# Scores of 16-column heads as products of 64 rows, with half as many masked copies of the keys and one set of three score banks

## The chip, the cores and the metric

The kernel runs on one core of one Trainium2 chip. The metric is the device time of one execution in microseconds (us), from the runs of this case. The engines are TensorE (PE in the profile, its weight loads PEld), VectorE (DVE), ScalarE (ACT), GpSimd (POOL) and SyncE (SP), which here only issues transfers.

## The reference, cut to what matters

64 images of 96x96 are cut into 36 patches each, so the tower works on 2304 tokens of D = 192 columns. It has an embedding, a first attention with 12 heads of 64 columns, an attention and MLP pair (`attn2`, `mlp`), a third attention (`attn3`) and a mixture of experts. The change touches `attn2` and `attn3` alone. Both have 12 heads of 16 columns over the 36 tokens of one image:

```
def _attn_branch(xp, w_qkv, w_proj, b_proj, ...):       # attn2, once per half of the images
    qkv = (xp @ w_qkv).reshape(B2, N, 3, H, hd).transpose(2, 0, 3, 1, 4)     # H = 12, hd = 16, N = 36
    a = softmax(einsum('bhnd,bhmd->bhnm', q, k) * hd ** -0.5)
    o = einsum('bhnm,bhmd->bhnd', a, v).transpose(0, 2, 1, 3).reshape(B2, N, C)
    o = o @ w_proj + b_proj
def _L1_attn_ref(x, w_qkv, b_qkv, w_proj, b_proj):      # attn3
    ...
    scores = einsum('bhnd,bhmd->bhnm', q, k) * scale + bias[None]            # bias: distance times slope
    attn = softmax(scores)
    out = einsum('bhnm,bhmd->bhnd', attn, v)
    ...
    return out @ w_proj.T + b_proj
```

## The kernel before

`narrow_stage` writes both stages, from one text; `attn2` has a normalisation in front (`prenorm`) and no bias on the scores, `attn3` has the bias and a normalisation behind (`postnorm`). Each engine runs its own program in order, and semaphores join them.

**Tiling.** A unit is two images (72 tokens), a group is four units (WIDE = 288 tokens). There are 32 units and 8 groups in a stage. The queries and keys of a group are projected into tiles with the columns of a head on 16 rows: `q_a` and `keys_a` hold heads 0 to 7 (128 rows), `q_b` and `keys_b` heads 8 to 11 (the rows 0 to 63 of a tile of 128, the rest zero).

**Scores of a unit.** A head uses 16 of the 128 rows of the array, so the keys stand in masked copies: copy h of `keys_a` is the keys with all rows but those of head h made zero. One product of the query (stationary, 64 columns of tokens, 36 of them of the image) with all copies (moving, 8 x 36 = 288 columns) then gives the scores of eight heads. `scores(k)` (L1020 on) does this for both images, a = 0 and 1, into the rows 0 to 63 and 64 to 127 of one bank of PSUM, then the same for `keys_b` with 4 x 36 = 144 columns. All matmuls here are f32 and appear in the trace as two records each. The masked copies are made by `mask_keys_a` on ScalarE (L1155 in `attn2`, L1157 in `attn3`), one instruction per copy, four in the step after the projection of the keys and four in the next; for the first group by one instruction of VectorE (`mask_keys_a0`, L1266 or L1267), and those of `keys_b` always by VectorE (`mask_keys_b`, the same lines).

**The order of a step.** The stage has 35 steps. In step k TensorE does `scores(k)`, `mix(k - 3)` (probabilities by values, L1060), a part of the next group's projections (j = k mod 4: transposes of the tokens L983 and L984; projections L994 to L998 of q_a and keys a; then q_b and keys b; then the values L1013 to L1017 in three parts), `turn(k - 2)` (four transposes of the probabilities, L1043) and `project_out` of the tiles that are ready (L1069, L1070). VectorE does `take_scores(k)` first: in `attn2` the row maximum (L1296) and its subtraction (L1298), both from PSUM; in `attn3` it adds the bias (L1290), takes the maximum (L1294), and GpSimd subtracts (L938). ScalarE takes the exponential (L1172), VectorE the row sums (L1305) and their reciprocals (L1310), GpSimd multiplies (L931), TensorE turns, ScalarE copies the turned probabilities out (`copy_turned`, L1179) and, after mix, z (L1189). In ScalarE's queue of a step stand: exponential of k - 1, copy of z, the work for the projections, copy of the turned, and last the mask copies.

**Buffers.** Scores have two banks (2 and 3), turned probabilities two (4 and 5), by the parity of k; so `scores(k)` waits until unit k - 2 is taken, and `turn(k)` until unit k - 2 is copied out. The first part of a group's values waits for all mask copies, since they read the bank that it writes.

## Time and profile before

| what | us |
|---|---|
| median of 3 timed runs | 906.39 (905.71 to 907.11) |
| the profiled execution, its own time | 909.75 |
| its span from first to last instruction | 908.0 |
| mean granted clock of TensorE | 0.965 |
| TensorE busy | 831.0 (92%) |
| VectorE busy | 543.1 (60%) |
| ScalarE busy | 461.0 (51%) |
| GpSimd busy | 410.3 (45%) |

The span is that of one execution under the profiler; what lies between it and the execution's time (1.75 us) is start and end. Busy times are unions of durations. The ends of matmuls are modelled, so the time that a matmul really holds TensorE is read from the start of one to the start of the next.

### The profile page before, as it was taken

What the parts mean: (1) busy time and instruction counts of PE and PEld (TensorE: products, weight loads), DVE (VectorE), ACT (ScalarE), POOL (GpSimd) and SP (SyncE); (2) the same over time, 40 slices, a digit from 0 to 9 for tenths busy, and PEclk for the clock granted to TensorE, in tenths of its full rate; (3) what the DMA queues carried; (4) which work ended last, traced back from release to release, by engine and by line L of the source; (5) the groups of instructions that cost most, each with busy time, mean ns of one, the idle gap of its engine ahead of it and who ended that gap; (6) DMA issues with size and microseconds to landing.
All of it is one profiled execution on the core that took longest, in us unless ns stands there. A gap on an engine that the chain in (4) does not pass through costs nothing. (4 is left out here: it accounts for less than half of the span.)

```text
span 908.0 us, 20892 instructions
## 1 busy us (share of the span) xinstructions
PE 831.0 (92%) x7511; PEld 748.5 (82%) x7511; DVE 543.1 (60%) x1466; ACT 461.0 (51%) x1150; POOL 410.3 (45%) x489
## 2 busy tenths in 40 slices
PE   9899999999998798998999988988979999999982
PEld 8889998899997577776999986776757899899972
DVE  2236555556665788884773326888875622466645
ACT  0346565555644587874345526877735221255533
POOL 1535444344444444432441225777851355244445
PEclk9989999999999999996999998999969999999997
DMA  9810111111110131214400002633200011233243
GB/s 315 255 50 21 22 35 37 31 31 30 38 36 2 33 67 25 37 19 123 74 1 1 1 26 42 138 68 68 42 7 2 29 62 63 76 103 100 83 149 116
DMA packets 103940, 55.75 MB, mean 61 GB/s; under 512 B 67264, under 2 KB 94512, under 8 KB 103840
## 3 DMA queue, kind: packets, MB, share of 16 engines
q1 hardware_dynamic: 98032, 43.04, 19.9%
q0 software_dynamic: 3792, 7.84, 2.5%
q10 hardware_dynamic: 2016, 3.54, 1.3%
q8 instruction: 62, 1.02, 0.5%
q14 instruction: 38, 0.31, 0.1%
HBM read 29.81 MB, written 13.97 MB: 48 GB/s over the span
## 5 line engine op out<-in xcount | busy, mean ns | idle before, releaser
L931 POOL TENSOR_TENSOR attn_prob<-attn_prob,attn_recip 100x432 f32<-100x432 f32 x64 | 58.6, 915 | 75.5 <-DVE attn_recip L1310 75.2
L450 POOL TENSOR_TENSOR attn_prob_x<-attn_prob,attn_recip 100x864 f32<-100x864 f32 x32 | 52.7, 1646 | 52.7 <-DVE attn_recip L759 52.7
L1886 POOL DMA_INDIRECT results<-moe_hid_shared x43 | 41.3, 960 | 58.4 <-ACT moe_hid_shared L2101 58.4
L1596 ACT ACTIVATE mlp_hid<-psum,columns 128x384 f32<-128x384 f32 x72 | 38.1, 579 | 41.4 <-PE psum L96 41.4
L1060 PEld LDWEIGHTS psum<-attn_prob_t,attn_values 108*64 108x64 f32 x1024 | 39.3, 142 | 13.6 <-ACT attn_prob_t L1179 7.8
L1060 PE MATMUL psum<-attn_prob_t,attn_values 108*64 108x36 f32 x1024 | 41.6, 228 | 6.1 <-ACT attn_prob_t L1179 4.1
L2076 ACT ACTIVATE moe_silu<-psum 128x384 f32<-128x384 f32 x36 | 17.7, 491 | 56.6 <-PE psum L107 56.6
L1033 PE MATMUL psum<-attn_keys_a,attn_q_a 128*64 128x288 f32 x256 | 45.8, 437 | 0.0
L1043 PE MATMUL psum<-ident,attn_prob 100*108 100x100 f32 x256 | 35.8, 265 | 9.5 <-POOL attn_prob L931 9.5
L1172 ACT ACTIVATE attn_prob<-attn_prob 100x432 f32<-100x432 f32 x64 | 36.5, 571 | 15.5 <-POOL attn_prob L938 14.7
L1305 DVE TENSOR_REDUCE attn_row_sum<-attn_prob 100x12 f32<-100x432 f32 x64 | 38.0, 594 | 8.1 <-ACT attn_prob L1172 7.9
L1549 PE MATMUL psum<-mlp_w_dn_s,mlp_hid 128*128 128x192 f32 (+2 forms) x306 | 42.6, 290 | 0.0
L436 POOL TENSOR_TENSOR attn_rstd<-attn_var_eps,neg_half 128x1 f32<-128x1 f32 x18 | 10.3, 570 | 71.3 <-DVE attn_var_eps L771 71.3
L686 ACT ACTIVATE attn_z_t<-psum 128x432 f32<-128x432 f32 (+2 forms) x32 | 16.2, 507 | 50.8 <-PE psum L566 50.7
L1549 PEld LDWEIGHTS psum<-mlp_w_dn_s,mlp_hid 128*128 128x128 f32 x306 | 42.0, 191 | 0.0
L938 POOL TENSOR_TENSOR attn_prob<-attn_prob,attn_row_max 100x432 f32<-100x432 f32 x32 | 29.2, 912 | 25.6 <-DVE attn_row_max L1294 25.6
L1964 PE MATMUL psum<-w_dn_shared,moe_hid_shared 128*128 128x192 f32 x216 | 36.3, 327 | 4.7 <-DVE moe_hid_shared L2251 3.3
L1964 PEld LDWEIGHTS psum<-w_dn_shared,moe_hid_shared 128*128 128x128 f32 x216 | 35.2, 190 | 5.4 <-DVE moe_hid_shared L2251 3.6
L576 PE MATMUL psum<-w_o,attn_z_t 128*128 128x192 f32 x216 | 38.7, 329 | 0.9 <-ACT attn_z_t L686 0.6
L1449 POOL TENSOR_TENSOR mlp_rstd<-mlp_var_eps,neg_half 128x1 f32<-128x1 f32 x18 | 10.6, 590 | 63.3 <-DVE mlp_var_eps L1665 63.3
L734 DVE TENSOR_SCALAR attn_k_diag<-psum,columns 64x288 f32<-64x288 f32 x48 | 25.0, 524 | 22.8 <-PE psum L508 15.4
L2251 DVE TENSOR_TENSOR moe_hid_shared<-psum,moe_silu 128x384 f32<-128x384 f32 x36 | 20.0, 555 | 30.8 <-PE psum L107 30.7
(473 smaller groups left out, 2853.5 us busy)
## 6 DMA issues: line engine op xcount, KB each, us to landing
embed_patches<-in_x SPq DMA_DIRECT2D x8, 768.0 KB, 17.2
sorted_rows<-mlp_pad_zeros SPq DMA_DIRECT2D x1, 4214.0 KB, 15.7
moe_hid_shared<-sorted_rows SPq DMA_DIRECT2D x43, 98.0 KB, 2.0
attn_v<-attn_v_tok SPq DMA_DIRECT2D x16, 216.0 KB
attn_values<-attn_v_tok SPq DMA_DIRECT2D x96, 27.0 KB
side_raw_a<-in_w_gu_dram SPq DMA_DIRECT2D x8, 288.0 KB, 3.3
side_raw_b<-in_w_gu_dram SPq DMA_DIRECT2D x16, 144.0 KB, 3.4
h_rows<-results SPq DMA_DIRECT2D x6, 288.0 KB, 5.3
```

The source lines that it names most:

```text
L450: nc.gpsimd.tensor_tensor(prob_x[k % 2][:, :, :, :], prob[k % 3][:, :, :].rearrange("p h (a n) -> p h a n", a=1) .to_broadcast([QP, HEADS, ...
L576: last = nc.tensor.matmul(out_ps, z_t[:, c, at:at + P], w_o[:, c, :], start=(c == 0), stop=(c == chunks - 1))
L931: nc.gpsimd.tensor_tensor(pr, pr, recip[k % 2][:, :].rearrange("p (h a) -> p h a", a=1) .to_broadcast([QP, HEADS, SEQ]), ALU.mult).then_in ...
L1033: last = nc.tensor.matmul(ps[64 * a:64 * a + 64, h0:h1, :], q[g % 2][:, at:at + 64], keys[g % 2][:, :, at:at + SEQ], start=True, stop=True)
L1043: last = nc.tensor.transpose(bank(4 + k % 2)[0:3 * SEQ, n * P:n * P + QP], flat[:, n * 3 * SEQ:(n + 1) * 3 * SEQ], ident[0:QP, 0:QP])
L1060: last = nc.tensor.matmul(ps[r:r + 64, n // 2, a * SEQ:(a + 1) * SEQ], v[:, n, :], prob_t[k % 2][:, n, a, :], start=True, stop=True)
L1172: nc.scalar.activation(prob[k % 3][:, :, :], prob[k % 3][:, :, :], ACT.Exp).then_inc(S["exp_done"], 1)
L1305: nc.vector.tensor_reduce(row_sum[:, :], prob[k % 3][:, :, :], axis=AX.X, op=ALU.add).then_inc(S["sum_ready"], 1)
L1549: last = nc.tensor.matmul(bank(3 + t)[:, 0:w.shape[1]], hid_step(n)[:, t * MT:(t + 1) * MT], w, start=(n == 0), stop=(n == 17), skip_group ...
L1596: nc.scalar.activation(hid_step(n), bank(n % 3)[:, 0:MW], ACT.Gelu, bias=b_up[:, c:c + 1]).then_inc(S["gelu_done"], 1)
L1886: nc.gpsimd.indirect_dma_start(out=results, out_offset=bass.IndirectOffsetOnAxis(ap=x_in[j % x_ring][:, D:D + 1].bitcast(U32), axis=0), in ...
L1964: last = nc.tensor.matmul(bank(4 + n % 2)[:, 0:D], hid_of(i)[:, c, t * P:(t + 1) * P], w_dn_shared[:, c, :], start=(c == 0), stop=(c == sh ...
```

## The change

The copies of `keys_a` are masked with period 64: copy h (0 to 3) keeps the rows of head h and of head h + 4, so there are four copies of 288 tokens and not eight. The rows 0 to 63 and 64 to 127 are then products of their own, of 64 rows by 64 columns of the array and 144 moving columns, for each of the two images: four products, of which each uses one quarter of the array. Heads 0 to 3 (rows 0 to 63), 4 to 7 (rows 64 to 127) and 8 to 11 (`keys_b`, products of 128 rows as before) go to three banks of their own, 2, 3 and 4. There is one such set, so `scores(k)` waits until unit k - 1 is taken. The turned probabilities keep bank 5 alone, so `turn(k)` waits until unit k - 1 is copied out. The reads of VectorE go over three banks with 144 columns each. A mask of four columns is made from that of eight at the start, by one more instruction of VectorE.

```diff
@@ -837,7 +837,7 @@
...
-    keys_a = [sb(f"keys_a{p}", [P, 8, WIDE]) for p in range(2)]
+    keys_a = [sb(f"keys_a{p}", [P, 4, WIDE]) for p in range(2)]
...
@@ -857,11 +857,10 @@
     def bank(b):
...
-    def scores_ps(k):
-        return bank(2 + k % 2)[:, 0:HEADS * SEQ].rearrange("p (h n) -> p h n", h=HEADS)
-
-    def turned_ps(k):
-        return bank(4 + k % 2).rearrange("p (g a n) -> p g a n", g=4, a=2)
+    scores_ps = psum[:, 2 * BANK:5 * BANK].rearrange("p (s n) -> p s n", s=3)[:, :, 0:4 * SEQ].rearrange(
+        "p s (h n) -> p s h n", h=4)
+
+    turned_ps = bank(5).rearrange("p (g a n) -> p g a n", g=4, a=2)
...
@@ -1000,7 +999,7 @@
...
         def values(g, n):
...
-                pe.wait_ge(S["keys_a_made"], 8 * g + 8)
+                pe.wait_ge(S["keys_a_made"], 4 * g + 4)
...
@@ -1021,26 +1020,28 @@
...
-                pe.wait_ge(S["keys_a_made"], 8 * g + 8)
+                pe.wait_ge(S["keys_a_made"], 4 * g + 4)
...
-            if k >= 2:
-                pe.wait_ge(S["scores_taken" if bias_hk is not None else "shifted"], k - 1)
-            ps = scores_ps(k)
-            for q, keys, h0, h1 in ((q_a, keys_a, 0, 8), (q_b, keys_b, 8, HEADS)):
-                for a in range(2):
-                    at = u * UNIT + a * SEQ
-                    last = nc.tensor.matmul(ps[64 * a:64 * a + 64, h0:h1, :], q[g % 2][:, at:at + 64],
-                                            keys[g % 2][:, :, at:at + SEQ], start=True, stop=True)
+            if k >= 1:
+                pe.wait_ge(S["scores_taken" if bias_hk is not None else "shifted"], k)
+            for r, a in ((0, 0), (64, 1), (0, 1), (64, 0)):
+                at = u * UNIT + a * SEQ
+                nc.tensor.matmul(scores_ps[64 * a:64 * a + 64, r // 64], q_a[g % 2][r:r + 64, at:at + 64],
+                                 keys_a[g % 2][r:r + 64, :, at:at + SEQ], start=True, stop=True)
+            for a in range(2):
+                at = u * UNIT + a * SEQ
+                last = nc.tensor.matmul(scores_ps[64 * a:64 * a + 64, 2], q_b[g % 2][:, at:at + 64],
+                                        keys_b[g % 2][:, :, at:at + SEQ], start=True, stop=True)
...
         def turn(k):
...
-            if k >= 2:
-                pe.wait_ge(S["turned_copied"], k - 1)
+            if k >= 1:
+                pe.wait_ge(S["turned_copied"], k)
...
-                last = nc.tensor.transpose(bank(4 + k % 2)[0:3 * SEQ, n * P:n * P + QP],
+                last = nc.tensor.transpose(bank(5)[0:3 * SEQ, n * P:n * P + QP],
...
@@ -1088,7 +1089,7 @@
...
-                keep_going(nc, bank(4), ident, out_ws[0][:, 0:2, :], 2)
+                keep_going(nc, bank(5), ident, out_ws[0][:, 0:2, :], 2)
...
@@ -1176,7 +1177,7 @@
...
-            nc.scalar.activation(prob_t[k % 2][:, :, :, :], turned_ps(k)[0:3 * SEQ, :, :, 0:SEQ], ACT.Copy
+            nc.scalar.activation(prob_t[k % 2][:, :, :, :], turned_ps[0:3 * SEQ, :, :, 0:SEQ], ACT.Copy
...
         def copy_z(k):
@@ -1218,9 +1219,9 @@
...
-                mask_keys_a(g, range(4))
+                mask_keys_a(g, range(2))
...
-                mask_keys_a(g, range(4, 8))
+                mask_keys_a(g, range(2, 4))
...
@@ -1270,7 +1271,7 @@
         def mask_keys_a0():
...
-                          None if qk_bias is None else qk_bias[:, 1:2]).then_inc(S["keys_a_made"], 8)
+                          None if qk_bias is None else qk_bias[:, 1:2]).then_inc(S["keys_a_made"], 4)
...
         def mask_keys_b(g):
...
@@ -1278,25 +1279,27 @@
...
             else:
...
-            spread_masked(keys_b[g % 2][0:DB, :, :], bank(0)[DB:P, 0:WIDE], head_mask[DB:P, 4:8],
+            spread_masked(keys_b[g % 2][0:DB, :, :], bank(0)[DB:P, 0:WIDE], head_mask[DB:P, :],
...
         def take_scores(k):
...
-            ps, pr, mx = scores_ps(k)[0:QP], prob[k % 3][:, :, :], row_max[k % 2][:, :]
+            ps, pr, mx = scores_ps[0:QP], prob[k % 3][:, :, :], row_max[k % 2][:, :]
+            pr_sets = pr.rearrange("p (s h) n -> p s h n", s=3)
             if bias_hk is not None:
-                nc.vector.tensor_tensor(pr, ps, bias_hk[:, :, :], ALU.add).then_inc(S["scores_taken"], 1)
+                nc.vector.tensor_tensor(pr_sets, ps, bias_hk[:, :, :].rearrange("p (s h) n -> p s h n", s=3), ALU.add
+                                        ).then_inc(S["scores_taken"], 1)
...
             else:
-                nc.vector.tensor_reduce(mx, ps, axis=AX.X, op=ALU.max).then_inc(S["max_done"], 1)
+                nc.vector.tensor_reduce(mx.rearrange("p (s h) -> p s h", s=3), ps, axis=AX.X, op=ALU.max).then_inc(S["max_done"], 1)
...
-                ins = nc.vector.tensor_tensor(pr, ps, mx.rearrange("p (h a) -> p h a", a=1)
-                                              .to_broadcast([QP, HEADS, SEQ]), ALU.subtract)
+                ins = nc.vector.tensor_tensor(pr_sets, ps, mx.rearrange("p (s h a) -> p s h a", s=3, a=1)
+                                              .to_broadcast([QP, 3, 4, SEQ]), ALU.subtract)
...
         def sum_up(k):
@@ -2647,7 +2650,7 @@
...
-        head_mask, k_bias_by_head3 = sb("head_mask", [P, 8]), sb("k_bias_by_head3", [P, 8])
+        head_mask, k_bias_by_head3 = sb("head_mask", [P, 4]), sb("k_bias_by_head3", [P, 4])
...
@@ -2682,6 +2685,7 @@
             def prepare(S, ssb):
...
+                head_mask8 = ssb("head_mask8", [P, 8])
...
@@ -2720,8 +2724,11 @@
...
                 def vector_start(dve):
...
-                    nc.vector.tensor_reduce(head_mask[:, :], ident[:, :].rearrange("p (h n) -> p h n", h=8),
+                    nc.vector.tensor_reduce(head_mask8[:, :], ident[:, :].rearrange("p (h n) -> p h n", h=8),
...
+                    dve.wait_ge(S["head_mask_ready"], 1)
+                    nc.vector.tensor_tensor(head_mask[:, :], head_mask8[:, 0:4], head_mask8[:, 4:8], ALU.add
+                                            ).then_inc(S["head_mask_ready"], 1)
...
@@ -2739,7 +2746,7 @@
                 def scale_columns(dve):
...
-                    dve.wait_ge(S["head_mask_ready"], 1)
+                    dve.wait_ge(S["head_mask_ready"], 2)
...
```

## Rows read from the trace of the kernel before

**Rows 1.** The page, busy time of the engines over the span.
```profile
PE 831.0 (92%) x7511; PEld 748.5 (82%) x7511; DVE 543.1 (60%) x1466; ACT 461.0 (51%) x1150; POOL 410.3 (45%) x489
```
**Rows 2.** Windows, one in `attn2` and one in `attn3`.
```profile
core 0: us, PE busy (x) PEld busy (x) DVE busy (x) ACT busy (x) POOL busy (x), PEclk, DMA share, GB/s
331.00:345.00 14.00, 13.71 (x160) 11.19 (x156) 12.63 (x32) 11.68 (x35) 6.35 (x9) 1.00 0.24 36
611.00:626.00 15.00, 13.63 (x158) 11.16 (x156) 14.12 (x30) 11.03 (x28) 10.83 (x13) 1.00 0.30 56
```
**Rows 3.** Timeline of TensorE in `attn2`: start, union of durations, instructions merged.
```profile
336.79 0.51 PE L1043 MATMUL psum<-ident,attn_prob 100*108 100x100 f32 x4
...
337.23 0.71 PE L1033 MATMUL psum<-attn_keys_a,attn_q_a 128*64 128x288 f32 x4
...
337.76 0.41 PE L1033 MATMUL psum<-attn_keys_b,attn_q_b 128*64 128x144 f32 x4
...
338.01 0.61 PE L1060 MATMUL psum<-attn_prob_t,attn_values 108*64 108x36 f32 x16
...
338.55 0.40 PE L994 MATMUL psum<-ring_a_hi,w_qkv_a_hi 128*128 128x288 f32 x1
...
343.84 0.51 PE L1043 MATMUL psum<-ident,attn_prob 100*108 100x100 f32 x4
...
344.19 0.51 PE L1069 MATMUL psum<-w_o,attn_z_t 128*128 128x192 f32 x2
...
344.95 0.71 PE L1033 MATMUL psum<-attn_keys_a,attn_q_a 128*64 128x288 f32 x4
```
**Rows 4.** Timeline around a mask batch: ScalarE, TensorE; last line `attn3`.
```profile
337.39 0.39 ACT L1179 ACTIVATE attn_prob_t<-psum 108x288 f32<-108x288 f32 x1
...
337.68 1.65 ACT L1155 ACTIVATE attn_keys_a<-psum,head_mask 128x288 f32<-128x288 f32 x4
...
339.22 0.57 ACT L1172 ACTIVATE attn_prob<-attn_prob 100x432 f32<-100x432 f32 x1
...
339.32 0.51 PE L1043 MATMUL psum<-ident,attn_prob 100*108 100x100 f32 x4
...
340.02 0.30 PEld L1069 LDWEIGHTS psum<-w_o,attn_z_t 128*128 128x128 f32 x2 [0.39 <-ACT attn_z_t L1189]
...
585.62 2.04 ACT L1157 ACTIVATE attn_keys_a<-psum,k_bias_by_head,head_mask 128x288 f32<-128x288 f32 x4
```
**Rows 5.** Waits of the weight loads, 303-415 and 551-671 us: total, times, longest.
```profile
PEld psum L1013 <- ACT attn_keys_a L1155: 1.9, 3, 0.9
...
PEld psum L1069 <- ACT attn_z_t L1189: 1.5, 4, 0.4
...
PEld psum L1043 <- POOL attn_prob L931: 4.4, 3, 1.7
PEld psum L1013 <- ACT attn_keys_a L1157: 4.4, 6, 1.3
...
PEld psum L1069 <- ACT attn_z_t L1189: 4.2, 5, 0.9
```
**Rows 6.** Instructions that write the key copies, VectorE: min/median/max ns, first and last start.
```profile
L1266 DVE TENSOR_TENSOR attn_keys_a<-psum,head_mask x1: 2558/2558/2558, 295.9 to 295.9; 128x2304 f32<-128x2304 f32 x1
...
L1266 DVE TENSOR_TENSOR attn_keys_b<-psum,head_mask x8: 1359/1359/1361, 298.5 to 398.5; 64x1152 f32<-64x1152 f32 x8
```
**Rows 7.** Timeline of TensorE at the two stages' starts: second part of the values.
```profile
300.02 0.31 PE L1013 MATMUL psum<-w_qkv_a_hi,ring_a_hi 128*108 128x192 f32 x1 [0.76 <-DVE attn_keys_b L1266]
...
548.25 0.32 PE L1013 MATMUL psum<-w_qkv_a_hi,ring_a_hi 128*108 128x192 f32 x1 [0.21 <-DVE attn_keys_b L1267]
```
**Rows 8.** Timeline: unit 7 taken, scores of unit 8; a wait in `attn3`.
```profile
330.08 0.61 DVE L1298 TENSOR_TENSOR attn_prob<-psum,attn_row_max 100x432 f32<-100x432 f32 x1
...
330.58 0.71 PE L1033 MATMUL psum<-attn_keys_a,attn_q_a 128*64 128x288 f32 x4
...
627.23 0.55 PE L1043 MATMUL psum<-ident,attn_prob 100*108 100x100 f32 x4 [1.39 <-POOL attn_prob L931]
```

## Prediction

> **What bounds the kernel now.** First the page's busy shares [rows 1]: TensorE works 92% of the span, VectorE 60%. That average hides the two stages that the change touches, `attn2` (about 294 to 430 us) and `attn3` (about 541 to 684 us), so the windows come next [rows 2]. There TensorE is busy 13.7 of 14 and 13.6 of 15 us, VectorE 12.6 of 14 and 14.1 of 15, ScalarE 11.7 and 11.0. A group of four units takes 14.4 us in `attn2` (scores of unit 8 at 330.58, of unit 12 at 344.95 [rows 8, 3]), and the three engines hand work to each other inside it. So the reader must look for who ends TensorE's waits, in the waits of its weight loads [rows 5], and for what lies on the way to them, in the timeline of one step [rows 3, 4]. Those waits, and the matmul time between them, are what the change can win.
>
> **Scores.** Today a unit's scores are two f32 products of 288 columns and two of 144, each recorded twice. Their pairs (a = 0, 1: two halves of the columns of the array) run abreast: the 288-column ones hold 0.53 us (337.23 to 337.76), the others 0.25 (337.76 to 338.01) [rows 3], 0.78 in all, 0.05 of it the uncovered first weight load (0.53 against twice 0.24). The change makes the first part four products of 64 rows and 144 columns. If all four run abreast they take what the 144-column pair takes, 0.24. The trace has no product of 64 rows, so this is bounded by the nearest rows: 0.24 four abreast, 0.48 two abreast, 0.96 one at a time. I take 0.24, since two products abreast with different moving data cost nothing today, and four half-height ones read no more rows and columns per moment. What is added is a change of shape between the quarters and the last two products. Its price, from the nearest rows: four transposes followed by a full product hold 0.35 us (343.84 to 344.19), followed by scores 0.44 (336.79 to 337.23) [rows 3], so 0.09, and 0.05 for the uncovered load: 0.14. Bounds 0 (if 64 and 128 rows don't count as different shapes) and 0.28 (a change among half-width shapes twice as dear); I take 0.15. New scores: 0.05 + 0.24 + 0.15 + 0.24 = 0.68, so 0.10 less a unit. For 64 units that is 6.4 us; TensorE sets the pace in some six of ten of them (elsewhere a wait behind takes the time back): **-3.8 us**, with bounds -9.6 (0.25 a unit in six of ten, no price for the switch) and +7.7 (two abreast, +0.15 a unit, on the path in eight of ten because TensorE is then later than the rest).
> That a change of shape costs 0.09 here agrees with the Trainium skill (TensorEngine Tiling, Key Properties), by which a change of tiling mode drains the array and a change of tile does not; this rule speaks against the change, and it has no figure. The Trainium skill (TensorE: Matmul & The Clock Gate, Part 3) gives a speedup of 3.07 for four row tiles, which no row here shows; an estimate from that page would make the quarters 0.31, the scores 0.75 and the whole term -1.2 (0.03 x 64 x 0.6) instead of -3.8.
>
> **Masks on ScalarE.** L1155 and L1157 write eight masked copies of the keys in each of seven groups, in two batches of four; the change makes them two batches of two. A batch of four holds 1.65 us in `attn2` (337.68 on), so two copies fewer take some 0.8 off. In `attn3` the batch is 2.04 [rows 4]; it loses some 1.0. In sum 14 x 0.8 + 14 x 1.0 = 25 us of ScalarE. Little of it is TensorE's: rows 4 show the way, mask batch, exponential 339.22, a copy of z, out projection 340.02, and TensorE's weight load had been waiting only 0.39 us. So the gain is capped by the waits that end on masks or on what is queued behind them [rows 5]: 1.9 + 1.5 us in `attn2`, 4.4 + 4.2 in `attn3`, 12.0 together. The wait for the normalised probabilities (4.4 in `attn3`) also hangs in part on an exponential behind a mask batch. VectorE, busy 0.90 and 0.94 of the windows, takes some back. I take six tenths of 12.0: **-7.2 us**, bounds -12 and -3.
>
> **Start of a stage.** The first group's masks are one VectorE instruction of 2304 columns, 2.56 us in `attn2`; of 1152 columns it is 1.36 [rows 6], 1.20 less. In `attn2` the second part of the values waits 0.76 for the key masks behind it (300.02), and the statistics that x_hat needs come after those on VectorE, so all 1.2 counts; in `attn3` TensorE came only 0.21 before them (548.25) [rows 7], so 0.2. **-1.4 us**; bounds -2.4 and -0.5.
>
> **One set of score banks.** scores(k) now waits for unit k-1 to be taken (L1298 in `attn2`, L1290 in `attn3`), before for k-2. Behind it in TensorE's queue stand mix, the projections and the transposes of k-2, for which ScalarE's and GpSimd's queues wait. I compared the end of each taking with the start of the next scores: of 62 pairs, 21 have less than 0.4 us between, twelve of them under 0.1. A usual one: taking ends 330.69, scores start 330.58 [rows 8]: 0.2 us of stall with the signal. The deep ones (scores up to 1.1 us ahead) come right before a wait for GpSimd, as the one at 627.23 of 1.39 us [rows 8], which absorbs them. Some seven stalls of 0.2: **+1.5 us**, bounds 0 and +10.5 (below).
>
> **At nothing.** One bank for turned probabilities: the copy out ends 337.78, the next transposes start 339.32 [rows 4]; the smallest such distance is 1.3 us; if ScalarE were that much later the transposes would wait by the rest. VectorE's score reads keep 432 columns, split over three banks; I take no change: L1298 takes 0.61 us for 432 columns [rows 8], 1.4 ns each, and L1266, which reads with one dimension more, 1.2 ns each [rows 6]. The extra mask addition at the very start lies beside the embedding loads. More instructions on TensorE (six products a unit for four) issue inside the stream: mix sends 16 in 0.54 us [rows 3].
>
> **Sum.** -3.8 - 7.2 - 1.4 + 1.5 = -10.9. The profiled execution took 909.75 us (span 908.0, 1.75 around it), so it would take 898.9; it stands 3.4 above the median of the timed runs, 906.39, and the same difference from that gives 895.5.
>
> **Rivals.** (1) The quarters do not run four abreast: slower. Two abreast: +7.7; masks only -5, as TensorE comes later to the waits; start -1.4, banks +1: +2.3, 908.7. One at a time: +0.62 a unit, about 935. It decides from 0.14 us more per unit than today ((1.4 + 7.2 - 1.5) over 64 x 0.8). For: no 64-row product in the trace. Against: today's pairs, with two streams of keys, overlap fully. (2) TensorE and VectorE in lockstep: the single set of banks eats what the masks give, since TensorE now arrives earlier at scores that VectorE has not taken. The 21 near pairs at 0.5 each: +10.5 for +1.5, 904.5. For: VectorE 0.94 busy in `attn3`. Against: VectorE's own start in those steps (row sum after exponential) lay behind the same mask batches. (3) The better case: no price for the switch (-9.6), masks -9, start -1.4, banks +1: -19, 887.4.
>
> **Numbers.** Forecast 0.55 (its own range 892 to 900); (1) 0.15; (2) 0.17; (3) 0.13. A measurement of this kernel can't tell 0.2% (1.8 us) from no change. Faster: 0.55 + 0.13 + 0.10 of (2) = 0.78; within 0.2%: 0.06 of (2) and 0.01 of (1) = 0.07; slower 0.15. The range goes from (3) to two abreast: 887 to 909.
>
> **What would show it.** The scores of a unit from first product to mix: 0.68 us right; 0.9 or more is (1). The start of the products after the quarters tells the switch. Mask batches of 0.9 and 1.1 us, and TensorE's waits for L1155 or L1157 nearly gone; if a group's pace in `attn2` stays 14.4 and TensorE waits for L1298 or L1290 in front of scores, it is (2). Transposes must not wait for L1179. Outside the two stages nothing may change. Wrong I would be by the quarters, or by a pace that VectorE alone sets.

## The result, and the profile after

| | before | changed |
|---|---|---|
| median of the session in which it was first timed, us | 907.22 | 902.24 |
| the profiled execution, us | 909.75 | 900.14 |
| its span, us; granted clock | 908.0; 0.965 | 898.4; 0.964 |

The changed kernel's median is that of 11 executions: a twelfth took 1054.58 us at a clock of 0.722 and is left out here and below. The ratio of the changed kernel to the one before is 0.9946 (95% interval 0.9926 to 0.9966), so 4.9 us less (3.1 to 6.7). Two later sessions gave 0.9949 (0.9928 to 0.9969) and 0.9964 (0.9947 to 0.9981). It is faster, and inside the range, but by 4.9 us and not by the forecast 10.9. The two profiled executions differ by more, 9.6 us. Two things have to be explained: what took the other 6 us, and why these two numbers disagree. In the rows below numbers of lines are those of the changed kernel: quarters L1030, the last two score products L1034, `turn` L1044, `mix` L1061.

The page's busy shares, and the two windows of [rows 2]:
```profile
PE 824.2 (92%) x7767; PEld 744.7 (83%) x7767; DVE 540.4 (60%) x1467; ACT 440.0 (49%) x1094; POOL 409.6 (46%) x489
```
```profile
core 0: us, PE busy (x) PEld busy (x) DVE busy (x) ACT busy (x) POOL busy (x), PEclk, DMA share, GB/s
331.00:345.00 14.00, 13.40 (x174) 11.00 (x172) 12.67 (x33) 10.14 (x29) 6.10 (x10) 1.00 0.24 36
611.00:626.00 15.00, 13.04 (x150) 10.94 (x150) 13.90 (x31) 8.32 (x22) 11.17 (x14) 0.89 0.27 46
```
ScalarE lost 21 us of work. TensorE's busy time fell in both windows, but in the second its clock is 0.89, where it was 1.00 in [rows 2].

One unit's scores in TensorE's timeline, to be held against [rows 3]:
```profile
335.68 0.51 PE L1044 MATMUL psum<-ident,attn_prob 100*108 100x100 f32 x4
336.12 0.48 PE L1030 MATMUL psum<-attn_keys_a,attn_q_a 64*64 64x144 f32 x8
336.53 0.47 PE L1034 MATMUL psum<-attn_keys_b,attn_q_b 128*64 128x144 f32 x4
336.82 0.61 PE L1061 MATMUL psum<-attn_prob_t,attn_values 108*64 108x36 f32 x16
```
The four quarters and the change of shape behind them hold 0.41 us (336.12 to 336.53), the other two products with the uncovered load 0.29: 0.70, against 0.78 before. Eight quarter records of about 0.3 us each lie within 0.48 us, so they run abreast (in the raw records their starts are 6 to 7 ns apart).

The writers of the key copies, by tile, and a batch on ScalarE in either stage (timeline):
```profile
L1156 ACT ACTIVATE attn_keys_a<-psum,head_mask x28: 482/494/504, 309.8 to 397.6; 128x288 f32<-128x288 f32 x28
...
L1267 DVE TENSOR_TENSOR attn_keys_a<-psum,head_mask x1: 1358/1358/1358, 295.9 to 295.9; 128x1152 f32<-128x1152 f32 x1
```
```profile
381.02 0.89 ACT L1156 ACTIVATE attn_keys_a<-psum,head_mask 128x288 f32<-128x288 f32 x2
```
```profile
577.99 1.07 ACT L1158 ACTIVATE attn_keys_a<-psum,k_bias_by_head,head_mask 128x288 f32<-128x288 f32 x2
```
These are the forecast 0.9, 1.1 and 1.36 us, for 1.65, 2.04 and 2.56 in [rows 4, 6].

Now who is waited for. The waits of the weight loads in `attn3` (541 to 661 us, which is the stretch of [rows 5] moved with the kernel), then those of the matmuls in `attn2` (303 to 415 us): total, times, longest.
```profile
PEld psum L1044 <- POOL attn_prob L930: 5.6, 7, 1.5
PEld psum L1061 <- DMA attn_values<-attn_v_tok: 3.5, 2, 2.0
...
PEld psum L1030 <- DVE attn_prob L1292: 1.3, 4, 0.5
```
```profile
PE psum L1030 <- DVE attn_prob L1301: 4.2, 8, 1.2
PE psum L1061 <- ACT attn_prob_t L1180: 3.7, 6, 1.4
```
No wait for L1158 over 0.4 us is left. New are the waits of the quarters for VectorE (L1301, L1292), which come from the single set of score banks. Those for the values' transfers are longer than before (here the row of the stretch of [rows 5]):
```profile
PEld psum L1060 <- DMA attn_values<-attn_v_tok: 2.6, 2, 1.5
```
For GpSimd the stretches don't compare well, since one wait of 3.3 us at the stage's end lies outside both. Over the whole stage (541 to 675 us) that wait holds 7.7 us before and 8.9 after.

**Where the 9.6 us lie.** Read from the starts of scores in the two traces, seven groups of `attn2` (units 0 to 28) take 101.60 us before and 101.67 after: no gain. Ahead of them 1.2 us are won (the start of the stage) and behind them 1.2 (units 28 to 31, where a stretch of half clock at 407 us stands before and not after). Seven groups of `attn3` take 105.77 and 101.09, and units 28 to 31 there 10.0 and 8.9. One more us lies between the two stages, where the change does nothing: the half-clock stretches that begin at 417 us last 17.1 us before and 13.7 after.

### The profile page after: what moved, and what is told of

Its sections match the earlier page's. It is cut to its first block and busy times, and to the rows that moved or that the text cites. A ratio compares the mean times of both kernels' runs of the same rounds, so it can differ in the third digit from the quotient of the medians.

```text
span 898.4 us, 21351 instructions
## 1 busy us (share of the span) xinstructions
PE 824.2 (92%) x7767; PEld 744.7 (83%) x7767; DVE 540.4 (60%) x1467; ACT 440.0 (49%) x1094; POOL 409.6 (46%) x489
## 5 line engine op out<-in xcount | busy, mean ns | idle before, releaser
L1061 PEld LDWEIGHTS psum<-attn_prob_t,attn_values 108*64 108x64 f32 x1024 | 39.5, 142 | 14.3 <-ACT attn_prob_t L1180 8.9
L1061 PE MATMUL psum<-attn_prob_t,attn_values 108*64 108x36 f32 x1024 | 41.6, 228 | 7.6 <-ACT attn_prob_t L1180 4.6
L1044 PE MATMUL psum<-ident,attn_prob 100*108 100x100 f32 x256 | 35.8, 265 | 8.4 <-POOL attn_prob L930 8.4
L436 POOL TENSOR_TENSOR attn_rstd<-attn_var_eps,neg_half 128x1 f32<-128x1 f32 x18 | 10.2, 568 | 71.3 <-DVE attn_var_eps L771 71.3
L553 PE MATMUL psum<-ident,attn_prob_x 100*72 100x100 f32 x384 | 38.4, 249 | 0.0
```

Source lines behind the costliest of these rows:

```text
L553: last = nc.tensor.transpose(bank(3 + p)[0:UNIT, n * P:n * P + QP], prob_x[k % 2][:, 4 * p + n, :, :].rearrange("p a n -> p (a n)"), ident ...
L1044: last = nc.tensor.transpose(bank(5)[0:3 * SEQ, n * P:n * P + QP], flat[:, n * 3 * SEQ:(n + 1) * 3 * SEQ], ident[0:QP, 0:QP])
L1061: last = nc.tensor.matmul(ps[r:r + 64, n // 2, a * SEQ:(a + 1) * SEQ], v[:, n, :], prob_t[k % 2][:, n, a, :], start=True, stop=True)
```

## The experiments

Ratios are to the kernel before, run on the same chip in the same session; 0.001 is 0.9 us. "Clock" is the median over a kernel's executions of the mean granted TensorE clock.

| kernel | ratio (95% interval) | median us | clock |
|---|---|---|---|
| changed, first session | 0.9946 (0.9926 to 0.9966) | 902.24 | 0.964 |
| e5, e14: changed again | 0.9949, 0.9964 | 903.20, 902.62 | 0.962 |
| e1 masks halved | 0.9968 (0.9950 to 0.9987) | 902.32 | 0.9665 |
| e2 wait for k-1 | 1.0033 (1.0010 to 1.0056) | 909.77 | 0.967 |
| e3 changed, masks doubled | 1.0040 (1.0020 to 1.0059) | 911.59 | 0.961 |
| e4 filler, 16 places | 0.9965 (0.9948 to 0.9982) | 902.70 | 0.970 |
| e6 masks halved and wait | 1.0000 (0.9981 to 1.0018) | 907.00 | 0.964 |
| e7 take earlier | 0.9974 (0.9951 to 0.9997) | 904.51 | 0.960 |
| e8 filler, 4 places | 0.9937 (0.9918 to 0.9957) | 900.41 | 0.9645 |
| e9 quarters last | 0.9964 (0.9937 to 0.9991) | 903.22 | 0.9675 |
| e10 before, filler, 4 places | 1.0012 (0.9994 to 1.0031) | 906.89 | 0.972 |
| e11 filler, 9 places | 0.9968 (0.9944 to 0.9993) | 903.19 | 0.9725 |
| e12 filler, 6 places | 0.9938 (0.9918 to 0.9958) | 899.04 | 0.9685 |
| e13 filler, 1 place | 0.9961 (0.9945 to 0.9977) | 901.70 | 0.967 |

### e1, e2 and e6: the masks alone, the wait alone, both, without quarters

e1 is the kernel before with four of ScalarE's eight copies from the third group on, which is six of the seven groups that ScalarE masks; the other four heads then use keys of an earlier group, so the output is another. e2 is the kernel before with the wait of the changed one. e6 has both edits.
```diff
-                mask_keys_a(g, range(4))
+                mask_keys_a(g, range(4 if g < 2 else 2))
...
-                mask_keys_a(g, range(4, 8))
+                mask_keys_a(g, range(4, 8 if g < 2 else 6))
...
-            if k >= 2:
-                pe.wait_ge(S["scores_taken" if bias_hk is not None else "shifted"], k - 1)
+            if k >= 1:
+                pe.wait_ge(S["scores_taken" if bias_hk is not None else "shifted"], k)
```


> The kernel before, with ScalarE writing only four of the eight copies of keys_a from the third group on (the other four stay as the group two before left them, so those heads' scores are of old keys). The scores keep their shape and their two banks. By the sum of the prediction the masks are worth -7.2 of the -10.9 us; six of seven groups have them here, so -6. The clock theory (what TensorE wins in these stages turns into idle stretches, in which its clock falls to half, and half of the win goes back) expects -3 to -4 on the median and a wide spread of the executions, as that of the changed kernel (895.6 to 907.4). The theory that the single set of banks takes the win expects the full -6, since both sets are here.

> The kernel before, with scores(k) waiting for unit k-1 to be taken instead of k-2: the wait of a single set of banks, without the quarters and with all eight mask copies. The prediction's term was +1.5 us (bounds 0 and +10.5). The bank theory expects +4 to +6, which would explain the gap between -10.9 forecast and some -5 measured; the clock theory expects +0 to +2.

> The kernel before with half of ScalarE's masked copies left out from the third group on (four heads' keys are those of an earlier group) and with scores(k) waiting until unit k-1 is taken; products of 128 rows as before. Theory lockstep: the one set of score banks gives back in attn2 what the masks won, so a clean group there (units 20 to 24) takes 13.8 us against 13.26 with the masks alone, TensorE idle ahead of the scores of its first unit, and the whole is 1 to 3 us under the kernel before. Theory clock: the wait alone is worth little, and the loss comes with the quarters; a clean group takes 13.3 and the whole is 5 to 6 us under before, as near as the mean clock lets it. The difference to the changed kernel is what the quarters do: forecast 3.8 us, under lockstep 1 to 2, since time saved ahead of a wait for VectorE lengthens the wait.

Measured: -2.9 us for the masks (-4.5 to -1.2), +3.0 for the wait (0.9 to 5.1), 0.0 for both (-1.7 to 1.6); the two add up. No theory has all three: e1 came out as the clock theory said, e2 between the two, and of e6 lockstep had the group (13.8 us) and its place for the wait, but not the whole. The masks are worth half of my -6 for six groups (-7.2 for seven), and the wait is twice my +1.5. A clean group of `attn2` at full clock (from the scores of unit 20 to those of unit 24) shows both. In order before, e1, e6, changed kernel, each as the window of the group and the row of the scores that end it:
```profile
374.65:388.33 13.68, 13.25 (x155) 10.88 (x154) 12.12 (x28) 11.18 (x32) 5.64 (x8) 1.00 0.23 32
...
388.33 0.71 PE L1033 MATMUL psum<-attn_keys_a,attn_q_a 128*64 128x288 f32 x4
```
```profile
371.13:384.39 13.26, 13.15 (x155) 10.83 (x154) 11.85 (x29) 9.95 (x28) 5.65 (x8) 1.00 0.24 33
...
384.39 0.71 PE L1033 MATMUL psum<-attn_keys_a,attn_q_a 128*64 128x288 f32 x4
```
```profile
371.55:385.36 13.81, 13.07 (x155) 10.99 (x155) 12.16 (x29) 10.28 (x29) 5.65 (x8) 1.00 0.23 32
...
385.36 0.71 PE L1033 MATMUL psum<-attn_keys_a,attn_q_a 128*64 128x288 f32 x4 [0.49 <-DVE attn_prob L1298]
```
```profile
374.05:387.79 13.74, 12.77 (x171) 10.57 (x171) 12.18 (x29) 10.24 (x29) 5.64 (x8) 1.00 0.23 33
...
387.79 0.48 PE L1030 MATMUL psum<-attn_keys_a,attn_q_a 64*64 64x144 f32 x8 [0.65 <-DVE attn_prob L1301]
```
The kernel before takes 13.68 for this group, TensorE idle 0.43 of it. The halved masks make it 13.26, with TensorE busy all but 0.11 of it. With the single set of banks it is 13.81: TensorE comes to a group's first scores before VectorE has taken the last unit of the group ahead, which stands in VectorE's queue behind a mask of 1.36 us and the normalisation of two token tiles. The quarters take 0.3 off TensorE's busy time, and the wait grows from 0.49 to 0.65; the group is 13.74. So in a clean group of `attn2` the whole change is worth nothing. Over seven groups the wait costs 1.7 us in `attn2` (98.20 in e1, 99.89 in e6) and 1.3 in `attn3` (103.86 and 105.20).

In `attn3` the masks' waits did go, and others grew. The waits of e1's weight loads, 546 to 666 us, against [rows 5]:
```profile
PEld psum L1043 <- POOL attn_prob L931: 11.1, 8, 3.3
...
PEld psum L1060 <- DMA attn_values<-attn_v_tok: 3.8, 2, 2.3
...
PEld psum L1013 <- ACT attn_keys_a L1157: 1.6, 2, 1.3
```
The wait for L1157 fell from 4.4 to 1.6 and that for the copy of z from 4.2 to nothing, 7.0 in all. The one for GpSimd rose from 4.4 to 11.1, but 3.3 of it is the wait at the stage's end that lay outside the stretch before: over the whole stage it is 7.7 before and 11.1 here, 3.4 more. The values' transfers took 1.2 more. So 4.6 of the 7.0 us came back as other waits.

### e3: the changed kernel with eight masked copies

ScalarE writes four further copies that nobody reads.
```diff
-                mask_keys_a(g, range(2))
+                mask_keys_a(g, (0, 1, 4, 5))
...
-                mask_keys_a(g, range(2, 4))
+                mask_keys_a(g, (2, 3, 6, 7))
```


> The changed kernel, with ScalarE writing eight copies in each group again (four of them are read by nobody). What is left is quarters, single set of banks and the shorter first mask. By the prediction's sum: -3.8 - 1.4 + 1.5 = -3.7 us against before. The bank theory expects no gain or a loss (-1.4 - 3.8 + 5 = 0); the clock theory -1 to -3.

Measured +3.6 us (1.8 to 5.3), outside what either theory expected: the quarters are worth nothing that can be measured when the masks are not halved. With e2 and e6 it makes a square, all with the wait for k-1, in us against before:

| | products of 128 rows | quarters and shorter start |
|---|---|---|
| eight copies | +3.0 (e2) | +3.6 (e3) |
| four copies | 0.0 (e6) | -4.3 (changed, mean of its three ratios) |

The quarters with the shorter start give 4.3 us where the masks are halved and -0.6 where they aren't; halving the masks gives 3.0 without quarters and 7.9 with them (without quarters in six of the seven groups alone). Each cell is uncertain by nearly 2 us, and e3's clock is the lower, 0.961 for e2's 0.967, so the size of this effect is rough and the clock's part in it is not separated. A reading that fits is that time saved on one engine of the three counts only when the next in line is out of the way as well.

### e9: what the change of shape costs

The two products of 128 rows go first, the quarters last.


> The changed kernel with the order of a unit's score products turned round: the two products of 128 rows first, then the four quarters, then mix. The number of changes between 64 and 128 rows ahead of a next product goes from one a unit (quarters to the other scores; the way in costs as before) to two. If a change costs the 0.11 to 0.16 us that was read between quarters and scores, a unit gets about 0.1 longer and the whole 2 to 6 us longer than the changed kernel, where TensorE sets the pace. If the gap after the quarters is not a price of the change of shape but of the order (a weight load that finds the array full), the unit takes 0.70 as before and the time stays.

Timeline of one unit (here L1030 is the pair of `keys_b`, L1034 the quarters):
```profile
384.62 0.47 PE L1030 MATMUL psum<-attn_keys_b,attn_q_b 128*64 128x144 f32 x4
385.02 0.47 PE L1034 MATMUL psum<-attn_keys_a,attn_q_a 64*64 64x144 f32 x8
385.43 0.66 PE L1061 MATMUL psum<-attn_prob_t,attn_values 108*64 108x36 f32 x16
```
The scores hold 0.81 us, 0.40 and 0.41, for 0.70: the pair that held 0.29 ahead of `mix` holds 0.40 ahead of the quarters. So one more change costs 0.11 us, whichever way it goes. Over 64 units that would be 7 us, yet the clean group takes only 13.84 instead of 13.74: TensorE waited 0.35 us for VectorE in front of the next group instead of 0.65. That is the same cushion seen from the other side. The whole is within its uncertainty of the changed kernel, of which no execution was timed beside it; the expected 2 to 6 us are neither shown nor excluded.

### e7: taking the scores earlier

```diff
-                if j == 2:
+                if j == 3:
                     pre_norm(g + 2)
```


> The changed kernel with one piece of VectorE's queue moved in attn2: the two normalising instructions L1250 go from a group's third step to its fourth, behind the taking of scores, so that the last unit of a group is taken 0.7 us earlier. Lockstep: TensorE's wait of 0.65 us ahead of the first scores of a group goes, a clean group takes 13.1 us instead of 13.74, and the whole is 3 to 5 us under the changed kernel. Clock: the idle is gone too, so the mean clock rises by 0.002 or more. If neither holds the pace stays 13.7 and the wait stands elsewhere (the transposes of x then wait for L1250).

The wait in front of the scores went, and the other one that I had named came:
```profile
389.76 0.30 PE L982 MATMUL psum<-ident,attn_x_hat 128*128 128x128 f32 x1 [0.54 <-DVE attn_x_hat L1250]
```
The clean group fell from 13.74 only to 13.31, and seven groups of the stage together took 101.8 us, as in the changed kernel (101.7); the whole did not gain (904.51 us, its clock 0.960). The expected 3 to 5 us and the higher clock did not come: moving one piece of VectorE's queue moved the wait to another place.

### The clock: e5, e14, e4, e8, e10, e11, e12, e13

The changed kernel's executions spread from 895.6 to 907.4 us (31 executions, three sessions) and follow their own mean clock: correlation -0.85, 0.69 us for each 0.001. For the kernel before (112 executions, four sessions) it is -0.87 and 0.52 us. The median clocks are 0.963 and 0.970. Read from the two fitted lines at a clock of 0.968, before takes 907.7 and the changed kernel 899.2: 8.5 us less, not 4.9.

The 8.5 us are less certain than they look: they compare kernels by straight lines through their executions, and 0.968 is above the clock of most executions of the changed kernel.

In the profile a lower mean is a few more stretches at half the clock (0.50, 1.2 GHz for 2.4). This is one of them, in the changed kernel, as windows and as the timeline ahead of it:
```profile
346.00:349.40 3.40, 1.77 (x32) 1.05 (x30) 1.88 (x5) 3.06 (x8) 1.40 (x2) 1.00 0.36 34
349.40:352.80 3.40, 3.40 (x15) 3.37 (x16) 2.84 (x9) 1.31 (x7) 1.27 (x2) 0.50 0.29 56
```
```profile
346.58 0.47 PE L1034 MATMUL psum<-attn_keys_b,attn_q_b 128*64 128x144 f32 x4
348.48 0.66 PE L1061 MATMUL psum<-attn_prob_t,attn_values 108*64 108x36 f32 x16 [1.43 <-ACT attn_prob_t L1180]
```
TensorE waits 1.43 us for the turned probabilities, is busy 1.77 of these 3.40 us, and then runs 3.4 us at 0.50. The kernel before has this wait too, of 1.35 us, and there the clock stays up:
```profile
346.40:349.80 3.40, 2.05 (x20) 1.45 (x22) 1.88 (x5) 2.86 (x7) 2.11 (x4) 1.00 0.36 37
349.80:353.20 3.40, 3.20 (x36) 2.86 (x38) 3.27 (x10) 2.33 (x9) 0.52 (x1) 1.00 0.29 29
```
At this place the clock fell in all six profiles of kernels with quarters and no filler (changed, e3, e5, e7, e9, e14) and in one of four without quarters (e2; not in before, e1, e6).

The test is work that takes the place of the idle time and computes nothing that is used, f32 products of 128 x 384 into a bank that is free. e8 has two of them at each of four waits, e13 at this one alone, e10 puts e8's into the kernel before, e4 has one in every group ahead of the mix of its third unit; e11 and e12 add further places.
```diff
+            if k >= 1:
+                pe.wait_ge(S["z_copied"], k)
+            if k in ((10, 14) if prenorm else (0, 8)):
+                keep_going(nc, bank(6), ident, out_ws[0][:, 0:2, :], 2)
             if u == 0:
                 pe.wait_ge(S[f"values_ready{g % 2}"], 16 * 9 * (g // 2 + 1))
             pe.wait_ge(S["turned_copied"], k + 1)
-            if k >= 1:
-                pe.wait_ge(S["z_copied"], k)
```
The filler writes the bank of z, so the wait for the copy of z moves ahead of it, in every step.


> The changed kernel once more, unaltered, on the chip of the three kernels beside it, so that they are compared with it in one session. Median 900 to 904 us, 4 to 6 us under the kernel before. In its profile each stretch of half clock inside the two stages should follow an idle time of TensorE, and executions with a lower mean granted clock should be longer by 1 to 2 us for each 0.002.

> The changed kernel, with one f32 product of 384 columns that nobody reads, in the bank of z, ahead of mix's wait for the turned probabilities in every fourth step (the one in which TensorE waits for ScalarE behind the rounding of the tokens). It takes 0.32 us twice of TensorE, in a place where it waits up to 1.4 us. If the clock takes the gain: fewer half-clock stretches inside the stages, mean granted clock above 0.966 in most executions, the spread narrower and the median 3 to 5 us below the changed kernel (897 to 899). If the clock has nothing to do with it: the same as the changed kernel or up to 3 us slower (16 fillers at 0.2).

> The changed kernel with two extra full products, 0.65 us together, at four places alone, each ahead of a wait in which TensorE stood idle for 0.96 to 1.73 us (the mixes of units 10 and 14 in attn2, 0 and 8 in attn3); no work of the kernel is changed. Clock: the stretches of half clock at 349 and 585 us go, the group that holds them gets 1.5 us shorter, the mean clock rises from 0.964 to 0.967 or more, and the whole is 2 to 4 us under the changed kernel with a smaller spread. Lockstep: no change, within 1 us of the changed kernel, since the waits stay as long.

> The changed kernel with two extra products at one place alone, ahead of the wait of 1.43 us in which TensorE stands idle in attn2 (the mix of unit 10). With the extra products at four places this group took 14.7 us instead of 16.25. If the half clock behind that wait is the price, this one place gives 1.0 to 1.8 us of the whole, 901 to 902, and the group of units 12 to 16 takes 14.7; if the gain of the four places came from elsewhere, the group stays at 16.25 and the time at the neighbour's.

> The changed kernel unaltered, a third time, as the neighbour of the two kernels beside it: 902 to 904 us, mean granted clock about 0.963.

e13 at the place shown, windows and timeline:
```profile
345.00:348.40 3.40, 3.40 (x38) 1.95 (x36) 1.91 (x5) 2.91 (x6) 1.69 (x3) 1.00 0.33 33
348.40:351.80 3.40, 3.20 (x32) 2.75 (x32) 3.24 (x11) 2.56 (x10) 1.00 (x2) 1.00 0.29 31
```
```profile
343.06 0.48 PE L1030 MATMUL psum<-attn_keys_a,attn_q_a 64*64 64x144 f32 x8 [0.27 <-DVE attn_prob L1303]
...
345.86 0.47 PE L1034 MATMUL psum<-attn_keys_b,attn_q_b 128*64 128x144 f32 x4
346.26 1.56 PE L337 MATMUL psum<-w_o,ident 128*128 128x384 f32 x4
347.76 0.66 PE L1063 MATMUL psum<-attn_prob_t,attn_values 108*64 108x36 f32 x16
...
357.74 0.47 PE L1030 MATMUL psum<-attn_keys_a,attn_q_a 64*64 64x144 f32 x8
```
Two products hold 1.5 us (I had expected 0.65), and `mix` still starts 1.90 us after the scores' last products, as without them. The clock stays at 1.00. The group from the scores of unit 12 to those of unit 16 takes 14.68 us (343.06 to 357.74). It took 16.25, 16.27 and 16.24 in the changed kernel's three profiles and 14.66 to 14.68 in e4, e8, e11, e12 and e13. So this one stretch of half clock costs 1.57 us, with nothing else changed but the filler. The kernel before takes 15.61 for the group. The change had made it 0.9 us shorter, and the clock turned that into 0.6 longer.

Over the whole the four places (e8) give -5.7 us against before, where the changed kernel gives -4.9, -4.6 and -3.3; the intervals overlap, and e8's clock, 0.9645, did not reach the expected 0.967. e4 missed: with one product at 16 places its clock rose to 0.970, that of the kernel before, and yet its median is 902.70 us for the 897 to 899 expected, the same as the changed kernel's. The one place (e13) gives nothing that can be told from its neighbour e14 (0.9961 and 0.9964), since stretches elsewhere come and go between executions: `attn3` has 10.2 us more of half clock in e13's profile than in the changed kernel's first.

> The kernel before with the same two extra products at the same four places, where its TensorE stands idle 0.85 to 1.35 us. Clock: the stretch of half clock at 561 us goes; there was none near 350 us in its profile, so less is to be won than in the changed kernel, 0 to 2 us, and its mean clock of 0.970 rises by at most 0.002. Had the extra products some other use, it would gain as much as the changed kernel, 3 us.

e10 gained nothing (1.0012), though its clock rose to 0.972. That fits a filler that helps only where a stretch of half clock stands on the path; the kernel before has none at the place shown.

> The changed kernel with the extra products of the four places and further ones ahead of five more waits: the first transposes of x in attn2 (idle 2.14 us), the scores of unit 20 in attn3 (1.96), the transposes of units 27, 29 and 30 in attn3 (1.40, 1.20 and 3.18). Clock: the stretches of half clock at 305, 619 and 660 us go or shrink, the mean clock reaches 0.972 or more and the time 895 to 898 us. If the clock has nothing to do with it, or the extra products run into the work behind them, 900 to 903 us.

> The changed kernel with extra products ahead of six waits (as in e11_more_fillers, but not at the end of attn3, where units 28 to 31 took 11.65 us with them instead of 8.88): the four of e8_filler_in_waits, the first transposes of x in attn2, and the scores of unit 20 in attn3. Clock: 898 to 900 us, 3 to 5 under its neighbour, the mean clock 0.968 or more, no stretch of half clock at 305, 349, 585 and 619 us. If extra products cost what they win, it stays at 902 to 904.

e11 is the warning. It has the highest clock of all, 0.9725, and no gain over the changed kernel. At the end of `attn3` its filler had to wait for the copy of z, ran at half clock itself and stood in front of the transposes:
```profile
647.84 2.92 PE L337 MATMUL psum<-w_o,ident 128*128 128x384 f32 x4 [1.36 <-ACT attn_z_t L1202]
```
Units 28 to 30 took 9.92 us between their scores, for 7.03. Without these places e12 has the fastest median of all, 899.04 us, ratio 0.9938 (0.9918 to 0.9958); it is the version to keep. Its six executions took 896.25 to 901.96 us and the twelve of the changed kernel beside it (e14) 900.09 to 906.31; the medians differ by 3.6 us, and resampled, the difference lies between 1.5 and 5.7 us in 95% of the draws, so this gain is clear of the noise. The ratios to the kernel before differ by less, 2.4 us. So filler wins 2.4 to 3.6 us in e12, less or nothing in e8 and e13, and in e4 and e11 nothing at all with a clock as high as the kernel before has. A higher mean clock is not a gain by itself, so the fit at 0.968 is evidence for the size of the clock's share, no proof.

One limit stays in e12. In `attn3` the mix of unit 8 waits for the values' transfers, first the changed kernel, then e12:
```profile
583.21 0.66 PE L1061 MATMUL psum<-attn_prob_t,attn_values 108*64 108x36 f32 x16 [1.73 <-DMA attn_values<-attn_v_tok]
```
```profile
581.56 0.66 PE L1063 MATMUL psum<-attn_prob_t,attn_values 108*64 108x36 f32 x16 [0.85 <-DMA attn_values<-attn_v_tok]
```
The wait before was 0.85 as well. It follows a stretch in which weights are loaded and the DMA engines are busy 90% or more (570 to 578 us in the changed kernel); I didn't try to move these loads, so that they are the cause is not shown.

## Why the prediction was right in direction and too large

**Scores, -3.8 us.** Right in its parts: four abreast, 0.70 us for the forecast 0.68. One change of shape costs 0.11 us by e9; of my 0.15 for it 0.05 was an uncovered load, which is there as well. It agrees with the Trainium skill (TensorEngine Tiling, Key Properties), by which changing the mode drains the array. The estimate of 0.75, worked out from the speedup of four row tiles in the Trainium skill (TensorE: Matmul & The Clock Gate, Part 3), was too dear by 0.05. The quarters, the shorter start and the seventh group's masks together measured -4.3 us (e6 to the changed kernel) for my -6.2 (3.8, 1.4 and a seventh of 7.2). In a clean group of `attn2` the quarters gave 0.07 us for the 0.24 that six of ten of 0.10 a unit would be, because VectorE's wait stood behind them.

**Masks, -7.2 us.** The batches have the durations forecast, and TensorE's waits for them went. But six groups of them are worth -2.9 us (e1; -4.5 to -1.2) for my -6.2. Scaled to seven this is an estimate of -3.4, hardly over my lower bound of 3. This is the term that failed by most. I took six tenths of the waits that end on masks, but did not ask for each what ends just behind it: of 7.0 us of such waits that went in `attn3`, 4.6 came back as waits for GpSimd's normalisation and the values' transfers.

**One set of banks, +1.5 us.** It measured +3.0 (e2; 0.9 to 5.1), and the same again from e1 to e6. I had counted about seven stalls, of 0.2 us each. The changed kernel's first profile has seven over 0.3 us, but of 0.84 on average (0.34, 0.56, 0.56, 0.65, 0.66, 1.15, 1.96). The count fits and the length was four times too short, though such a stall doesn't cost its full length: the seven are 5.9 us, the cost 3.0. I had taken the length from one usual pair; that TensorE comes earlier once the masks are halved explains only a part, since e2 has all the masks and five stalls over 0.3 us, of 0.69 on average.

**Rival 2, lockstep.** By its own signs it is what happened in `attn2`. The group of units 8 to 12, 14.4 us before, takes 14.2 (329.55 to 343.78), TensorE waits for L1301 in front of scores, and in e6 the single set of banks takes back all that the masks gave, 0.0 for -2.9. Six of the ten waits stand at the first scores of a group. Its price was too high: ten waits and 6.5 us in all, not 21 of 0.5.

**The sum.** The three measured parts, -2.9, +3.0 and -4.3, give -4.2 us. The last is the remainder from e6 to the changed kernel, so the only independent test in it is that e1 and e2 add up to e6. So the failed step is the six tenths of the masks' waits: 3.3 of the missing 6.7 us. The banks' stalls are 1.5, and the quarters with the rest 1.9. Each of these has an uncertainty of about 2 us.

**What the sum had no term for.** The last line carried a difference worked out from one trace over to the median ("the same difference from that"). The kernel's executions have a mean clock of 0.970 before and 0.963 after, and 0.007 would be worth 3.6 to 4.8 us at 0.52 to 0.69 us for 0.001. Read from the fitted lines at a clock of 0.968, the parts are masks -5.2 (902.5 against 907.7), wait +1.5 (909.2), and quarters with the rest -5.8 (899.2 against e6's 905.0); the changed kernel itself is -8.5, not far from the forecast 10.9. This also fits the two profiled executions, at 0.965 and 0.964, which differ by 9.6. So part of each miss above may be clock. Shown are the price of one such stretch in place, 1.57 us, and the 2.4 to 3.6 us that e12 wins with filler; e4 and e11, where a clock of 0.970 and more won nothing, speak against the whole of it. How the missing 6 us divide between new waits and clock stays open.

**The start, -1.4 us.** First projection to first scores fell from 6.82 to 5.62 us in `attn2` (the -1.2 forecast) and from 8.13 to 7.88 in `attn3` (0.2 forecast). The second agreement is luck. In the changed kernel's profile a stretch of half clock of 6.8 us begins just ahead of this start. In e3, e4, e9 and e11, which have the same start and a stretch of 3.4 us there, it takes 6.93, so there too 1.2 us are won; the kernels with the longer first mask (before, e1, e2, e6, e10) take 8.13 with either.

**The rest.** The transposes never waited for the single bank of turned probabilities. Rival 1, quarters that don't run abreast, is refuted by their starts; rival 3 needed a free change of shape. Outside the two stages the profiles differ by 1 us, in stretches of half clock.

## What to carry to other kernels

Before adding up waits that an edit removes, find for each the next event that TensorE would wait for, and read slack from a timeline in which the removed work is already gone. Price a wait that a smaller buffer adds from the longest stalls that it can bring, not from a usual one. When an edit shortens TensorE's work but not the waits of other engines, the saving becomes idle time, and in one place here the clock took it back: compare executions by granted clock as well as by median, and put filler into long waits only where it neither waits for anything itself nor stands ahead of ready work.

## What was not expected of the hardware

The same place, with an idle wait of 1.23 to 1.43 us, kept the clock at 1.00 in three kernels (before, e1, e6) and lost it in seven; the wait's length does not tell them apart, since before and e6 kept it and e2 lost it with 1.35 us in all three. One stretch at 0.50 cost 1.57 us of 3.4. A change between products of 64 and of 128 rows costs 0.11 us in either direction, while four quarters with two different sets of keys and queries start within 20 ns of each other.
